# A new timetable for the side work of an attention and spiking feed-forward kernel

## The chip, the core and the metric

The kernel runs on one core of a Trainium2 chip. A core has five engines that run their own instruction streams and meet only through semaphores: TensorE (PE, matrix products into PSUM), VectorE (DVE), ScalarE (ACT), GpSimd (POOL) and SyncE (SP, here only a DMA queue). Data lie in SBUF (128 partitions) and in PSUM (eight banks of 128 x 512 floats). The metric is the device time of one launch in microseconds, lower is better; it is given as the median of several runs.

## What is computed

For each of 32 sequences of 256 tokens and 128 features, in f32:

```python
xn  = layernorm(x)
h   = layernorm(xn) * ln_scale + ln_bias
c_q, c_kv = h @ w_down_q.T, h @ w_down_kv.T            # 64 latents each
q, k, v = (c_q @ w_up_q.T), (c_kv @ w_up_k.T), (c_kv @ w_up_v.T)   # 16 heads of 64
q, k = rope(q), rope(k)
attn = softmax(q @ k.T / 8)                            # 256 x 256 for each head
att_out = (attn @ v) @ w_out.T + xn
y   = relu(xn @ W_fc.T)**2 @ W_proj.T                  # 512 hidden units
spikes = number of firings in 5 steps of a leaky integrator driven by y, / 5
out = x + att_out + spikes
```

The top-k of the reference's attention is computed there but not returned, and is not needed.

## The kernel before

A sequence is a batch b; its 16 heads are 8 pairs. One step handles one pair at each stage of a software pipeline, so there are 32 x 8 = 256 steps, plus 12 to fill the pipeline and 8 to drain it. In the text a step has the number p = 0 to 7 within its batch, and g is the running number of the pair. The table `LEAD` says how far ahead of the current pair each stage works: project 12, rope 10, scores 8, turn 7. Each engine has a function `step(i, s)` that issues its part of one step in a fixed order written out by hand, and `run` calls it: some steps written out ahead, a loop whose body is two batches (16 steps), then the last body and the drain written out.

The main stages of one step, engine by engine:

- PE: `scores` of pair g+8 (8 matmul records into one of two halves of ps_s), `project` of pair g+12 (into the one bank ps_qk, from the latents of that batch, once ACT has copied the pair before out of it), the side work (`extras`), and `weigh_latents` of pair g (8 records into the one bank ps_u).
- DVE: `row_max` of g+8, `rotate` of g+12 (times the cosines, ps_qk to qk), side work, `turn` of g+7 (32 x 32 transposes of the exponentials), side work.
- ACT: `exponentials` of g+8 (four of them), `copy_projected` of g+12 (ps_qk to raw), in every odd step `exchange` (two DMAs that swap neighbouring rows of two pairs, raw to partner), side work, `copy_u` of g.
- POOL: `add_rotated` of g+10, two instructions (partner times the sines; added to qk), then side work. It waits for the exchange by DMA of its two pairs. In step p it handles pair p+10, so the pairs 16 and 17, exchanged by ACT in step 5, are POOL's in steps 6 and 7, and PE needs them for the scores of steps 0 and 1 of the batch after.
- SP: after the turn of every fourth pair (in steps 0 and 4), `move`: 16 DMAs of 128 KB, turned to gathered, which `weigh_latents` reads four steps later.

The side work of a batch, with the step p in which each engine has it before the change:

- The input chain works two batches ahead: load x (SP 0), `moments_of` (DVE 0), `inverse_std` (POOL 0), `normalise` twice (ACT 1), `transpose_inputs` (PE 2), `copy_inputs` (ACT 2), `latents` (PE 3), `lead_latents` (ACT 3), `split_latents` (DVE 3); the first `project` that reads the result is PE's in step 4. `residual` (POOL 3) adds x to xn in place.
- `latents_by_token` of batch b+1 (PE 1) and `copy_latents` (ACT 1).
- Feed forward: `ffn_in` half 0 of b+1 (PE 7) and half 1 of b (PE 0), `relu` (ACT 7, 0), `square` (POOL 1, 2), `ffn_out` (PE 4, 5), `integrate` (DVE 5, 6).
- Softmax sums: `invert_sums` (DVE 4), `split_sums` (POOL 5), `transpose_rden` (PE 7), `copy_rden` (ACT, first of step 0 of the batch after), then `broadcast_rden` and `normalise_u` of that batch's steps 0 to 3.
- Output of batch b-1: `attention_out` in four parts (PE 4, 5, and two in 6), `add_spikes` (DVE 7), `transpose_sum` (PE 7), `finish` (DVE 7), `store` (SP).

All input and feed-forward products share the one bank ps_a; the sums and the output share ps_b.

## Time and profile before

| | |
|---|---|
| median of 3 runs (lowest to highest) | 1379.97 us (1379.85 to 1381.91) |
| the profiled execution | 1372.12 us, its span 1370.3 us |
| mean granted TensorE clock | 0.951 of 2.4 GHz |
| busy: PE, DVE, ACT, POOL | 81%, 72%, 61%, 59% of the span |
| DMA engines, mean busy share and rate | 62% in the steady part, 159 GB/s over the span |
| one batch in the steady part | 41.0 us |

The profiled execution is a run of its own and 7.9 us shorter than the median. Busy shares are unions of instruction records; PE's matmul records overlap, so its share is an upper reading. A record of f32 matrix products comes twice, since the product is issued as two instructions. The timeline of a stretch gives for each engine the start of an instruction and, in brackets, how long the engine had been idle before it and what ended that; the time an instruction holds its engine is best read from one start to the next start, since the records of neighbouring instructions overlap by some 0.1 us.

### The profile page before, as it was taken

How to read it: one execution, taken by the hardware profiler on the slowest of the kernel's cores; microseconds unless marked ns; L12 is line 12 of the kernel's file. 1: busy time of each engine (PE TensorE's matmuls, PEld its weight loads, DVE VectorE, ACT ScalarE, POOL GpSimd, SP SyncE). 2: the span in 40 equal slices, each digit the busy share in tenths (PEclk: the TensorE clock that was granted, in tenths of full speed). 3: DMA queues.
4: the chain of work that ended last, by engine and by line, in shares of the span. 5: the costliest groups of instructions: out<-in, count | busy, mean ns of one | idle time of the engine just before them, and what ended most of it. 6: DMA issues, size and time to landing. Idle time of an engine off the chain costs nothing.

```text
span 1370.3 us, 25645 instructions
## 1 busy us (share of the span) xinstructions
PE 1103.4 (81%) x6880; PEld 741.2 (54%) x6880; DVE 981.3 (72%) x1350; ACT 840.0 (61%) x2945; POOL 806.7 (59%) x837
## 2 busy tenths in 40 slices
PE   3677788887788887788887788887788887788886
PEld 2445555555555555555555555555555555555554
DVE  3667777677777777777677777676778676778672
ACT  2566666666665666665666665666665666666650
POOL 3567656557656557656556656556656556755640
PEclk9889999999999999999999999999999999999998
DMA  4456665665665665665665675565575565576562
GB/s 143 119 149 162 183 169 149 178 159 147 176 174 147 173 162 149 171 178 149 167 168 146 168 180 154 160 172 148 162 180 159 155 173 151 158 181 162 153 171 54
DMA packets 93273, 217.87 MB, mean 159 GB/s; under 512 B 22464, under 2 KB 43200, under 8 KB 93120
## 3 DMA queue, kind: packets, MB, share of 16 engines
q1 hardware_dynamic: 72768, 150.45, 47.1%
q10 hardware_dynamic: 20480, 67.13, 13.2%
q8 instruction: 11, 0.18, 0.1%
q14 instruction: 14, 0.11, 0.0%
HBM read 7.77 MB, written 4.19 MB: 9 GB/s over the span
## 4 chain that ended last, share of the span: by engine, by line
PE 37%; issue 17%; ACT 16%; DVE 15%; ACTq 7%; POOL 5%; SPq 1%; DMA 1%; DVEq 0%; POOLq 0%
PE ps_s L300 9%; PE ps_u L314 9%; ACT prob L473 9%; DVE neg_max L596 7%; ACTq L493 7%; PE ps_b L390 6%; PE ps_a L365 4%; ACT raw L485 3%; PE ps_qk L290 3%; DVE turned L605 3%; POOL partner L730 2%; PE ps_a L352 2%; POOL qk L733 2%; DVE count L649 2%; DVE qk L591 2%
## 5 line engine op out<-in xcount | busy, mean ns | idle before, releaser
L473 ACT ACTIVATE prob<-ps_s,neg_max 128x256 f32<-128x256 f32 x1024 | 472.3, 476 | 308.2 <-DVE neg_max L596 308.2
L730 POOL TENSOR_TENSOR partner<-partner,rope_sb 128x512 f32<-128x512 f32 x256 | 326.9, 1277 | 472.9 <-DMA partner<-raw 472.3
L596 DVE TENSOR_REDUCE neg_max<-ps_s 128x4 f32<-128x1024 f32 x256 | 312.2, 1220 | 203.0 <-PE ps_s L300 201.0
L733 POOL TENSOR_TENSOR qk<-qk,partner 128x512 f32<-128x512 f32 x256 | 325.7, 1272 | 20.1
L605 DVE STREAM_TRANSPOSE turned<-prob 128x1024 f32<-128x1024 f32 x256 | 314.1, 1227 | 0.9
L300 PE MATMUL ps_s<-qk 64*128 64x256 f32 x2048 | 296.5, 409 | 13.8 <-POOL qk L733 12.4
L314 PE MATMUL ps_u<-gathered,ckv 128*64 128x256 f32 x2048 | 280.6, 395 | 5.7 <-DMA gathered<-turned 3.7
L290 PE MATMUL ps_qk<-latent,wup_hi 128*128 128x256 f32 x512 | 173.4, 358 | 123.5 <-DVE latent L638 98.5
L300 PEld LDWEIGHTS ps_s<-qk 64*128 64x128 f32 x2048 | 179.6, 189 | 126.6 <-issue 80.1
L290 PEld LDWEIGHTS ps_qk<-latent,wup_hi 128*128 128x128 f32 x512 | 105.5, 206 | 215.2 <-issue 149.5
L473 ACT ACTIVATION_READ_ACCUMULATOR prob<-ps_s,neg_max 128x1 f32 x1024 | 211.1, 206 | 0.0
L314 PEld LDWEIGHTS ps_u<-gathered,ckv 128*64 128x64 f32 x2048 | 125.1, 137 | 115.2 <-issue 69.2
L591 DVE TENSOR_TENSOR qk<-ps_qk,rope_sb 128x512 f32<-128x512 f32 x256 | 174.2, 681 | 8.9 <-PE ps_qk L291 8.7
L485 ACT COPY raw<-ps_qk 128x512 f32<-128x512 f32 x256 | 153.4, 599 | 9.1 <-DVE qk L591 9.1
L390 PE MATMUL ps_b<-u_n,wvo_sb 128*128 128x256 f32 x512 | 154.4, 443 | 0.8 <-DVE u_n L619 0.8
L291 PE MATMUL ps_qk<-latent,wup_lo 128*128 128x256 f32 x512 | 144.4, 301 | 0.0
L501 ACT COPY u_raw<-ps_u 128x256 f32<-128x256 f32 x256 | 98.8, 386 | 68.0 <-issue 39.9
L390 PEld LDWEIGHTS ps_b<-u_n,wvo_sb 128*128 128x128 f32 x512 | 107.3, 226 | 16.4 <-issue 2.1
L619 DVE TENSOR_TENSOR u_n<-u_raw,ps_b 128x512 f32<-128x512 f32 x128 | 86.9, 679 | 32.6 <-PE ps_b L382 32.6
L291 PEld LDWEIGHTS ps_qk<-latent,wup_lo 128*128 128x128 f32 x512 | 107.9, 211 | 0.0
L638 DVE TENSOR_TENSOR latent<-ps_a,latent 64x256 fp32r<-64x256 f32 x64 | 27.0, 422 | 101.5 <-ACT latent L527 101.1
L382 PE MATMUL ps_b<-rden_t,sel_sb 128*128 128x256 f32 x256 | 55.5, 298 | 41.4 <-ACT rden_t L545 38.8
(57 smaller groups left out, 906.3 us busy)
## 6 DMA issues: line engine op xcount, KB each, us to landing
gathered<-turned SPq DMA_DIRECT2D x1024, 128.0 KB, 2.8
partner<-raw ACTq DMA_DIRECT2D x256, 256.0 KB, 2.6
x_sb<-in_x SPq DMA_DIRECT2D x32, 128.0 KB, 2.2
resid<-xn_sb SPq DMA_DIRECT2D x32, 128.0 KB, 2.0
out<-out_sb SPq DMA_DIRECT2D x32, 128.0 KB, 1.9
turned<-in_wup SPq DMA_DIRECT2D x2, 512.0 KB, 5.8
rope_sb<-in_rope SPq DMA_DIRECT2D x1, 512.0 KB, 6.9
turned<-in_wo_t SPq DMA_DIRECT2D x1, 512.0 KB, 8.2
```

The source lines that it names most:

```text
L290: nc.tensor.matmul(bank, wup_hi[:, which, cols], rhs, start=True, stop=False)
L291: last = nc.tensor.matmul(bank, wup_lo[:, which, cols], rhs, start=False, stop=True)
L300: last = nc.tensor.matmul(ps_s[:, s % 2, h, t, :], qk[rows, s % 4, 0, t * P:(t + 1) * P], qk[rows, s % 4, 1, :], start=True, stop=True)
L314: last = nc.tensor.matmul(ps_u[h * L:(h + 1) * L, 0:S], ckv[:, (s // PAIRS) % 2, kt, :], gathered[:, (s // GROUP) % 2, :, s % GROUP, h, kt ...
L390: last = nc.tensor.matmul(ps_b[:, 0:S], wvo_sb[:, pair, :], u_n[:, pair, :], start=(pair == 0), stop=(pair == PAIRS - 1))
L473: last = nc.scalar.activation(prob[:, s % 2, :, h, :, t, :].rearrange("p j k c -> p k j c"), ps_s[:, s % 2, h, t, :].rearrange("p (k j c) ...
L485: nc.scalar.copy(raw[:, duo % 2, s % 2, :, :], ps_qk[:, :, :]).then_inc(raw_ready, 1)
L591: nc.vector.tensor_tensor(qk[:, s % 4, :, :], ps_qk[:, :, :], cos_sb, ALU.mult).then_inc(cos_ready, 1)
L596: nc.vector.tensor_reduce(neg_max[:, s % 2, :, :], ps_s[:, s % 2, :, :, :], AXIS_X, ALU.max, negate=True).then_inc(max_ready, 1)
L605: nc.vector.transpose(turned[:, par, :, s % GROUP, :], prob[:, s % 2, :, :, :, :, :].rearrange("p j h k t c -> p j (h k t c)"))\
L730: nc.gpsimd.tensor_tensor(other, other, sin_sb, ALU.mult).then_inc(sin_ready, 1)
L733: nc.gpsimd.tensor_tensor(qk[:, s % 4, :, :], qk[:, s % 4, :, :], other, ALU.add).then_inc(rope_done, 1)
```

## The change

The side work gets new steps, the order within a step changes in places, and four buffers change with it.

- Input chain: now three batches ahead at its head. `load_x` of b+3 (SP 0), `moments_of` b+3 (DVE 2), `inverse_std` (POOL 3), `normalise` (ACT 4 and 5, one each), `transpose_inputs` b+3 (PE 7), `copy_inputs` (ACT 7), then of b+2: `latents` (PE 0), `lead_latents` (ACT 0), `split_latents` (DVE 1). `residual` of b+2 moves to POOL 4.
- `latents_by_token` and `copy_latents` of b+1 move from step 1 to step 0, into another part of ps_a.
- Feed forward: `ffn_in` of b+1 in PE 5 and 6, `relu` ACT 5 and 6, `square` POOL 6 and 7, `ffn_out` PE 2 and 3, `integrate` DVE 3 and 4.
- Sums: `invert_sums` from DVE 4 to 5, `split_sums` from POOL 5 to 6 (behind `square`, and behind `add_rotated`, which stands first in POOL's step). `transpose_rden` stays in PE 7.
- Output: `attention_out` one part in each of steps 4 to 7; `finish` is the first thing of DVE's step 0 of the batch after; `store` and `keep_residual` in SP 3. `broadcast_rden` comes behind the other extras of its step.
- Buffers: h_t gets two halves; `residual` writes a new buffer `early`, not xn_sb in place. Waits are added to match (`latent_split`, `relu_done`, `ckv_ready`, `ckv_mm`, `moments_ready`, `res_ready`).
- Prologue: the statistics of x of batch 1 (`moments_of`, `inverse_std`) are made there. The loop runs one body less and the last two bodies are written out; the drain has nine steps.

The core of the diff:

```diff
@@ run
-            with eng.Fori(1, B // UNROLL - 1) as i:
+            with eng.Fori(1, B // UNROLL - 2) as i:
...
-            for s in range(PAIRS):
+            for s in range(PAIRS + 1):
@@ SP step
-                if p == 0:
-                    if not outside(b, B):
-                        sp.wait_ge(res_ready, done(b))
-                    if not outside(b, B) and not outside(b + 2, B):
-                        load_x(b + 2, b0)
+                if p == 0 and not outside(b + 1, B) and not outside(b + 3, B):
+                    sp.wait_ge(res_ready, done(b + 1))
+                    load_x(b + 3, 1 - b0)
+                if (s + turn) % GROUP == GROUP - 1 and not outside(g + turn, STEPS):
+                    move(g + turn, s + turn)
+                if p == 3:
...
@@ PE extras
+                if not outside(b - 1, B) and p >= 4:
+                    attention_out(b - 1, p - 4)
+                if p == 0:
+                    if not outside(b + 2, B):
+                        latents(b + 2, b0)
+                    if not outside(b + 1, B):
+                        latents_by_token(b + 1, 1 - b0)
+                if not outside(b, B) and p in (2, 3):
+                    ffn_out(b, p - 2)
+                if not outside(b + 1, B) and p in (5, 6):
+                    ffn_in(b + 1, p - 5, 1 - b0)
+                if p < 4 and not outside(b - 1, B):
+                    broadcast_rden(b - 1, p)
+                if p == 7:
+                    if not outside(b + 3, B):
+                        transpose_inputs(b + 3, 1 - b0)
+                    if not outside(b - 1, B):
                         transpose_sum(b - 1)
...
                     if not outside(b, B):
                         transpose_rden(b)
@@ ACT step
+                if p == 0:
+                    if not outside(b + 2, B):
+                        lead_latents(b + 2, b0)
+                    if not outside(b + 1, B):
                         copy_latents(b + 1, 1 - b0)
+                if not outside(b + 1, B) and p in (5, 6):
+                    relu(b + 1, p - 5)
+                if not outside(b + 3, B):
+                    if p in (4, 5):
+                        normalise(b + 3, 1 - b0, p - 4)
                     elif p == 7:
...
+                        copy_inputs(b + 3, 1 - b0)
@@ DVE step
+                if p == 0 and not outside(b - 2, B):
+                    finish(b - 2, b0, i - 1)
...
-                if p == 0 and not outside(b + 2, B):
-                    moments_of(b + 2, b0, i + 1)
-                elif p == 3 and not outside(b + 2, B):
+                if p == 1 and not outside(b + 2, B):
                     split_latents(b + 2, b0)
-                elif p == 4 and not outside(b, B):
+                elif p == 2 and not outside(b + 3, B) and not outside(b + 1, B):
+                    moments_of(b + 3, 1 - b0, i + 1 + b0)
+                elif p == 5 and not outside(b, B):
                     invert_sums(b, b0)
...
-                    if p == 5:
+                    if p == 3:
                         for k in (0, 1):
                             integrate(b, b0, k)
-                    elif p == 6:
+                    elif p == 4:
@@ POOL step
                 if not outside(g + LEAD["rope"], STEPS):
                     add_rotated(g + LEAD["rope"], s + LEAD["rope"], i)
-                if p == 0 and not outside(b + 2, B):
-                    inverse_std(b + 2)
-                if p in (1, 2) and not outside(b, B):
-                    square(b, p - 1)
-                if p == 3 and not outside(b + 2, B):
-                    residual(b + 2, b0)
-                if p == 5 and not outside(b, B):
+                if p == 3 and not outside(b + 3, B) and not outside(b + 1, B):
+                    inverse_std(b + 3)
+                if p == 4 and not outside(b + 2, B):
+                    residual(b + 2, b0, i + 1)
+                if p in (6, 7) and not outside(b + 1, B):
+                    square(b + 1, p - 6)
+                if p == 6 and not outside(b, B):
                     split_sums(b)
```

## Rows read from the trace of the kernel before

**Rows 1.** The page: busy time and share of the span of each engine.
```profile
PE 1103.4 (81%) x6880; PEld 741.2 (54%) x6880; DVE 981.3 (72%) x1350; ACT 840.0 (61%) x2945; POOL 806.7 (59%) x837
```

**Rows 2.** Instructions of copy_rden, one in each batch: first and last start.
```profile
L545 ACT CAST rden_t<-ps_b x9: 390/390/391, 354.6 to 682.3; 128x256 fp32r<-128x256 f32 x9
```

**Rows 3.** Who waited for whom over the whole span: total us, times, longest.
```profile
PE ps_qk L290 <- DVE latent L638: 98.5, 32, 3.3
```

**Rows 4.** Timeline, steps 2 to 4: start, duration, engine, line, [idle before].
```profile
693.05 0.41 PE L326 MATMUL ps_a<-ident_sb,z_sb 128*128 128x128 f32 x2 [2.09 <-ACT z_sb L513]
...
701.44 0.86 DVE L638 TENSOR_TENSOR latent<-ps_a,latent 64x256 fp32r<-64x256 f32 x2 [3.22 <-ACT latent L527]
...
702.43 0.58 PE L290 MATMUL ps_qk<-latent,wup_hi 128*128 128x256 f32 x1 [3.21 <-DVE latent L638]
```

**Rows 5.** Stretches of 2 us: busy of PE, PEld, DVE, ACT, POOL, then clock, DMA, GB/s.
```profile
692.00:694.00 2.00, 0.95 (x8) 0.74 (x10) 1.29 (x2) 2.00 (x8) 0.00 (x0) 1.00 0.98 240
...
702.00:704.00 2.00, 1.57 (x6) 1.49 (x7) 1.94 (x3) 0.00 (x0) 1.73 (x3) 0.58 0.00 0
```

**Rows 6.** Timeline, PE: end of step 4, and step 5 without a wait.
```profile
706.40 1.08 PE L314 MATMUL ps_u<-gathered,ckv 128*64 128x256 f32 x8
707.41 1.13 PE L300 MATMUL ps_s<-qk 64*128 64x256 f32 x8
708.48 0.38 PE L290 MATMUL ps_qk<-latent,wup_hi 128*128 128x256 f32 x1
...
709.05 1.02 PE L390 MATMUL ps_b<-u_n,wvo_sb 128*128 128x256 f32 x4
...
710.87 1.08 PE L314 MATMUL ps_u<-gathered,ckv 128*64 128x256 f32 x8
711.88 1.13 PE L300 MATMUL ps_s<-qk 64*128 64x256 f32 x8
```

**Rows 7.** Timeline, DVE, step 6.
```profile
713.07 1.23 DVE L596 TENSOR_REDUCE neg_max<-ps_s 128x4 f32<-128x1024 f32 x1 [0.73 <-PE ps_s L300]
714.21 0.68 DVE L591 TENSOR_TENSOR qk<-ps_qk,rope_sb 128x512 f32<-128x512 f32 x1
714.80 1.24 DVE L605 STREAM_TRANSPOSE turned<-prob 128x1024 f32<-128x1024 f32 x1
715.96 1.30 DVE L649 SCALAR_TENSOR_TENSOR count<-ps_a,count 128x256 f32<-128x256 f32 x3
```

**Rows 8.** Timeline, ACT, step 5 and the first exponential of step 6.
```profile
709.85 0.47 ACT L473 ACTIVATE prob<-ps_s,neg_max 128x256 f32<-128x256 f32 x1 [1.88 <-DVE neg_max L596]
...
711.67 0.60 ACT L485 COPY raw<-ps_qk 128x512 f32<-128x512 f32 x1
712.29 1.12 ACTq L493 DMA_DIRECT2D partner<-raw  x2
713.46 0.37 ACT L501 COPY u_raw<-ps_u 128x256 f32<-128x256 f32 x1 [1.19 <-issue]
714.33 0.48 ACT L473 ACTIVATE prob<-ps_s,neg_max 128x256 f32<-128x256 f32 x1 [0.50 <-DVE neg_max L596]
```

**Rows 9.** Timeline: the move of step 4 on SP, POOL, and PE's transpose_rden.
```profile
697.99 1.04 POOL L770 TENSOR_TENSOR relu_sb<-relu_sb 128x512 f32<-128x512 f32 x1
...
706.88 5.58 SPq L245 DMA_DIRECT2D gathered<-turned  x9
...
707.63 0.21 POOL L762 CAST rden_hl<-rden 128x32 fp32r<-128x32 f32 x1
707.92 0.25 POOL L764 TENSOR_TENSOR rden_hl<-rden,rden_hl 128x32 fp32r<-128x32 f32 x1
...
717.88 1.28 POOL L730 TENSOR_TENSOR partner<-partner,rope_sb 128x512 f32<-128x512 f32 x1 [9.71 <-DMA partner<-raw]
...
718.23 0.38 PE L374 MATMUL ps_b<-ident_sb,rden_hl 128*128 128x128 f32 x2
...
719.23 1.28 POOL L733 TENSOR_TENSOR qk<-qk,partner 128x512 f32<-128x512 f32 x1
```

**Rows 10.** The exchange DMAs over two batches: from issue to landing.
```profile
DMA to landing us min/median/max: 2.2/2.7/5.2
```

More of the change, by code:

```diff
@@ L270, in step @@
                     if not outside(b, B):
+                        sp.wait_ge(res_ready, done(b))
                         keep_residual(b0)
[L272 to L273 removed]
             run(sp, prologue, step)
```

96 lines of the change are left out of this document (32 added, 64 removed).

## Prediction, made before the run

> **What bounds the kernel now.** I read the busy shares first: PE 81%, DVE 72%, ACT 61%, POOL 59% [rows 1]. No engine is full, so the time is set by who waits for whom. Next I took the spacing of an instruction that comes once in a batch: eight periods in 327.7 us, 40.96 us a batch [rows 2]. The table of waits names the largest wait of PE: project behind the latents of the next batch but one, 98.5 us in 32 times, so 3.1 us in every batch [rows 3]. The timeline shows the place: in step 3 the products of the latents, their copy on ACT and their split on DVE follow one another within one step; the split starts at 701.44, after DVE has been idle for 3.22 us, and PE's project of step 4 at 702.43, after 3.21 us [rows 4]. In the same way PE stood 2.09 us in step 2 for the normalised input [rows 4].
>
> The wait costs more than itself. After it TensorE's clock is at the lower of its two levels: 0.58 in the stretch from 702 to 704 [rows 5]. The same work (project, one part of attention_out, half of ffn_out) takes 3.97 us from 702.43 to 706.40 [rows 4, 6], and in the next step, at the full clock, 2.39 us from 708.48 to 710.87 [rows 6]. So 1.6 us more, 4.8 us in all. After the shorter wait of 2.09 us the clock stayed at 1.00 [rows 4, 5].
>
> Then I read a step without such a wait, from start to start. PE: scores 1.07, project 0.57, two groups of four side products 1.82, weigh 1.01; 4.47 in all from 707.41 to 711.88 [rows 6]. DVE: row_max 1.14, rotate 0.59, turn 1.16 [rows 7]. ACT: four exponentials 1.82, then the copy of the projection; the copy with the exchange behind it holds ACT for 1.79, without one about 0.48 (the 0.60 record less the overlap of 0.1) [rows 8]. From scores' start to row_max is 1.19 [rows 6, 7], from row_max to the first exponential 1.26 [rows 7, 8].
>
> **The change part by part.** Hardly any work is added or taken away: no product, no exponential. What changes is who waits. I lay the new order out by hand for one batch, with these durations, and put zero at the start of row_max in step 1.
>
> DVE leads in steps 1 to 4. Step 1 has row_max, rotate, normalise_u (as long as rotate, 0.6) and the split (0.86 [rows 4]) and the turn: 1.14 + 0.6 + 0.6 + 0.9 + 1.2 = 4.4. Step 2 has the moments instead of the split; their instructions don't stand in my rows, and I take 0.8, the split's price (at least 0.4, the price of one small DVE instruction, at most 1.3, that of three compares [rows 7]): 4.4. Step 3 has two compares of integrate, at 1.30 / 3 = 0.43 each [rows 7]: 4.4. Step 4 has three and no normalise_u: 4.2. So row_max of step 5 is at 17.4. PE's own load is 2.9 to 3.8 in these steps, with ffn_out and broadcast in steps 2 and 3, and ACT's at most 3.9; both fit beneath DVE. The latents are split in step 1 and read in step 4, three steps of slack, so the wait of 3.21 us and the slow clock behind it go. The input is normalised in steps 4 and 5 and transposed in 7, so the 2.09 us wait goes as well. This is the gain: 3.2 + 1.6 + 2.1 = 6.9 us of PE in a batch, before one asks what is late next.
>
> Next comes ACT. In step 5 it has exponentials 1.8, copy with exchange 1.8, a relu 0.5, a normalise of two instructions 0.8 and copy_u 0.25: 5.15. It begins at 17.4 + 1.3 = 18.6 and is free at 23.8, where the maxima of step 6 have been ready since 22.8. That 1.0 us is the first new wait. PE's weigh of step 6 needs copy_u of step 5 and ends at 25.0.
>
> PE in step 7: scores to 26.1, project 0.6, the last part of attention_out 0.86, transpose_inputs 0.6, a wait of 0.2 for add_spikes, transpose_sum 0.2. It comes to transpose_rden at 28.6. If rden were there, the next step's first scores would end at 31.0, the load of PE's step 0 (1.07 + 0.57 + 0.43 + 0.48 + 0.24 + 1.1, with a wait of 0.4 for copy_inputs) would follow, and row_max of the next step 1 would be at 35.4. That is a batch of 35.4 us.
>
> But rden isn't there. This is the step on which I settle. split_sums moves on POOL from step 5 to step 6 and so behind add_rotated of pair 16 and behind a square. POOL handles its instructions in order, and add_rotated of pair 16 waits for the exchange which ACT issues in step 5, in the middle of the 16 DMAs of the move of step 4. Now the rows: the move began at 706.88, the copy of the projection at 711.67, the exchange at 712.29, and POOL could start only at 717.88, after 9.71 us idle [rows 8, 9]. That is 6.2 us after the copy, where a landing of the median 2.7 instead of 5.2 [rows 10] would give 3.7. In the kernel before split_sums had been done at 708.2, while POOL waited for nothing; PE's transpose_rden at 718.23 came before POOL was through with pair 16, at 720.5 [rows 9]. With the old spacing of steps the new place of split_sums alone would be some 4 us too late.
>
> In my timetable: row_max of step 5 at 17.4, exponentials 18.6, copy 20.4, POOL on pair 16 at 26.6 (the exchange falls 4.7 us into the move; before 5.4 us, so as contended), 2.6 for the two instructions (717.88 to 719.23 and 1.28 [rows 9]), 29.2; square 1.0 [rows 9], 30.2; split_sums 0.54 (707.63 to 708.17 [rows 9]), 30.8. PE has then waited 2.2 us. It goes on: transpose 0.3, weigh 1.0, so step 0 starts at 32.1; its load is 3.9 (the wait for copy_inputs is covered now); 36.0; row_max of step 1 1.2 later, 37.2. The chain closes, and DVE, free at 36.9, isn't late. A batch of 37.2 us.
>
> POOL's other dates: pair 12 is contended in the same way by the move of step 0 (copy of step 1 at 3.1, POOL at 9.2, done 11.8; scores want it at 10.9, but DVE takes them only at 13.1, which hides it: free, and up to 1 us a batch if DVE were faster). inverse_std in step 3 then ends at 16.6, just as ACT's normalise comes at 16.7; 0.8 us of slack on ACT hides a late one. SP: load_x and its wait for residual stand ahead of the move of step 0, but the residual was added in step 4 of the batch before, so the move isn't held. store and keep_residual come behind the move, done issuing at about 10 (16 DMAs at 0.62 [rows 9]), and residual needs the copy at 19. The move itself is issued at -0.3 and read at 14; it took about 11 us before, so 3 us of slack. Added semaphore waits on DVE (moments_ready, ckv_ready) and ACT (ckv_mm, res_ready) are for things one step or more old: 0 each, at most 0.1 for each of the four. One body written out more costs nothing that I can see; I put 0 to 3 us in all on it.
>
> Sum. Taking 0.2 for the small handovers, 37.4 us against 40.96 in each of 30 batches (pairs of the batches 0 to 29; in the last two no exchange is left in step 5): 106 us. In the filling steps one wait of 4.8 goes, and the moments of batch 1 in DVE's prologue add 0.8: 4 us less. The drain is one step longer but has the same chain: 0, up to 2 either way. 1372.1 - 110 = 1262 for a profiled execution; the median of the runs stood 7.9 above that before, so 1270.
>
> **The rivals.**
>
> A, the forecast: 1270, with its own range 1250 to 1290 (a landing 0.6 us earlier or later for each batch is 18 us). For it: the 9.71 us idle of POOL ahead of exactly that pair.
>
> B: the new wait of 2.2 us in step 7 pulls TensorE's clock to its lower level. The rows have a wait of 2.09 us that didn't and one of 3.21 us that did [rows 4, 5]; mine lies nearer the first. The price is the 1.6 us from above: 39.0 us a batch, 1318. The Trainium skill (TensorE: Matmul & The Clock Gate, section Why this matters for your kernels) warns against idle gaps between bursts of matmuls since they send the clock back to 1.2 GHz; by that rule this timetable is at risk wherever it leaves one long gap, and the trace bears the rule out at 702 us.
>
> C: the exchange isn't held up, since the moves lie otherwise, and rden is in time: 35.4 us a batch, 30 x 5.55 + 4 = 170 less, 1210. Against it: both contended exchanges of a batch had the same delay, at 3.6 and 5.4 us into a move. The Trainium skill (DMA: Bandwidth & Descriptors, section Issuing engines are not separate DMA queues) says the DMAs of all issuing engines run on the same 16 engines and interleave, which leaves no room for C unless the move is over.
>
> D, slower than before: the exchange of step 5 is served only when the move has drained. In the rows its end at 717.88 is 11.0 us after the move's start, which could be the move's own end. Then it lands 11 - 4.7 + 2.7 = 9.0 us after its issue instead of 5.6, PE waits 5.6 us, the clock falls (1.6): 37.4 + 3.4 + 1.6 = 42.4 us, 1420. It turns the sign from about 2.1 us more delay on, if the clock falls too. Against it: the other contended exchange of the same batch was through while the DMA engines were still full.
>
> E: the waits only change their names and nothing is gained; 1380. Nothing in the load of the engines (at most about 31 us in a batch) speaks for it.
>
> **How the numbers follow.** A 0.64, B 0.17, C 0.12, D 0.05, E 0.02. The predicted time is A's, 1270. Range 1235 to 1330: A and B with room for the unknown costs; C and D stay out. A measurement of this kernel can tell about 0.2% from no change. Faster by more than that 0.91 (all but D, E and a rest of B), within it 0.02, slower 0.07.
>
> **What the profile should show.** The wait of project for the latents and its clock of 0.58 gone; the mean clock at 0.98 or more (B: about 0.95); a wait of PE at transpose_rden (L374's successor) for POOL's second instruction of split_sums, some 2.2 us, about 30 times; POOL still idle ahead of pair 16 for the exchange; DVE's wait for scores mostly in steps 7, 0 and 1. In steps 1 to 4 steps of 4.2 to 4.4 us with DVE nearly full, about 5.1 on ACT in step 5, and a batch of 37.4 us. It would be wrong if transpose_rden doesn't wait (C), if the wait is over 3 us (B, D), or if DVE isn't the leader of steps 1 to 4.

## The result and the profile after

The changed kernel takes 1252.76 us, the median of 4 runs (1250.01 to 1256.78), against 1379.91 us (1379.67 to 1381.91) for the kernel before. The ratio is 0.908 with the interval 0.905 to 0.910. Predicted were 1270 us, with a range of 1235 to 1330, and 1250 to 1290 for the forecast by itself. The profiled execution took 1253.07 us; its span is 1251.3 us and the mean granted clock 0.982, where it was 0.951.

The page of the profile after, busy time and share of the span of each engine, answers to [rows 1]. DVE, ACT and POOL work as long as before, within 1.1 us; their shares have risen since the span is shorter.

```profile
PE 1074.8 (86%) x6880; PEld 712.4 (57%) x6880; DVE 982.4 (79%) x1350; ACT 840.9 (67%) x2945; POOL 807.0 (64%) x837
```

The table of waits after (total us, times, longest) answers to [rows 3]. Project's wait for the split of the latents, 98.5 us in 32 times before, is left once, with 2.4 us. In its place stand PE's waits for POOL's second instruction of split_sums, 30 times and 43.6 us, so 1.45 us in a batch. Project's waits for ACT's copy of the pair before have grown from 25.0 to 58.1 us.

```profile
POOL partner L727 <- DMA partner<-raw: 353.8, 68, 8.7
...
DVE neg_max L589 <- PE ps_s L302: 159.9, 106, 8.5
...
PE ps_qk L292 <- ACT raw L481: 58.1, 99, 3.5
...
PE ps_b L377 <- POOL rden_hl L763: 43.6, 30, 5.7
```

The timeline of one batch after (start, duration, engine, line, and in brackets the idle time before) shows the chain that the prediction had laid out by hand. It answers to [rows 8, 9]. ACT copies the projection in step 5 at 612.37 and issues the exchange; the move of step 4 has been running since 608.33; POOL gets the exchanged pair only at 618.45; then come its second instruction, a square and split_sums; and transpose_rden on PE starts at 622.62, after an idle of 1.58 us.

```profile
608.33 10.95 SPq L247 DMA_DIRECT2D gathered<-turned  x16
...
612.37 0.60 ACT L481 COPY raw<-ps_qk 128x512 f32<-128x512 f32 x1
613.00 1.22 ACTq L489 DMA_DIRECT2D partner<-raw  x2
...
618.45 1.28 POOL L727 TENSOR_TENSOR partner<-partner,rope_sb 128x512 f32<-128x512 f32 x1 [3.79 <-DMA partner<-raw]
619.81 1.27 POOL L730 TENSOR_TENSOR qk<-qk,partner 128x512 f32<-128x512 f32 x1
621.04 1.03 POOL L769 TENSOR_TENSOR relu_sb<-relu_sb 128x512 f32<-128x512 f32 x1
622.03 0.20 POOL L761 CAST rden_hl<-rden 128x32 fp32r<-128x32 f32 x1
622.31 0.25 POOL L763 TENSOR_TENSOR rden_hl<-rden,rden_hl 128x32 fp32r<-128x32 f32 x1
...
622.62 0.44 PE L377 MATMUL ps_b<-ident_sb,rden_hl 128*128 128x128 f32 x2 [1.58 <-POOL rden_hl L763]
```

To see where the time went I took the start of every row_max on DVE, from that of pair 16 to that of pair 240 (28 batches), and worked out the mean length in us of each of the eight steps, from one row_max to the next. The step lengths and batches of all the other kernels below are taken over the same 28 batches. Steps count as in the kernel's description; "hand" is the timetable of the prediction, each step rounded by itself.

| step | 0 | 1 | 2 | 3 | 4 | 5 | 6 | 7 | batch |
|---|---|---|---|---|---|---|---|---|---|
| before | 5.28 | 3.49 | 6.12 | 7.81 | 4.95 | 4.47 | 4.47 | 4.32 | 40.92 |
| after | 3.87 | 4.61 | 4.29 | 4.25 | 4.11 | 4.19 | 4.72 | 6.87 | 36.91 |
| hand | 3.9 | 4.4 | 4.4 | 4.4 | 4.2 | 4.1 | 4.7 | 7.2 | 37.2 |

The gain comes from steps 2, 3, 0 and 4 (1.8, 3.6, 1.4 and 0.8 us); 1.1 us are given back in step 1, which took over the split, and 2.5 in step 7, where PE waits for the sums. 4.01 us a batch, 30 times, are 120 us; the profiled executions differ by 119.

### The profile page after: what moved, and what is told of

It reads as the page before. It is cut to its first block, busy times and chain, and to the rows that moved or that the text cites. A ratio compares the mean times of both kernels' runs of the same rounds, so it can differ in the third digit from the quotient of the medians.

```text
span 1251.3 us, 25664 instructions
## 1 busy us (share of the span) xinstructions
PE 1074.8 (86%) x6880; PEld 712.4 (57%) x6880; DVE 982.4 (79%) x1350; ACT 840.9 (67%) x2945; POOL 807.0 (64%) x837
## 3 DMA queue, kind: packets, MB, share of 16 engines
HBM read 7.77 MB, written 4.19 MB: 10 GB/s over the span
## 4 chain that ended last, share of the span: by engine, by line
issue 46%; POOL 37%; DVE 7%; PE 6%; SPq 1%; POOLq 1%; DMA 1%; DVEq 0%; ACT 0%; ACTq 0%
POOL partner L727 17%; POOL qk L730 10%; POOL relu_sb L769 4%; POOL rstd L742 2%; POOL early L753 2%; PE ps_u L316 2%; DVE turned L598 2%; DVE neg_max L589 2%; PE ps_s L302 1%; DVE u_n L612 1%; DVE qk L584 1%; PE ps_b L393 1%; SPq L247 1%; DMA x_sb<-in_x 1%; POOL var_eps L737 1%
## 5 line engine op out<-in xcount | busy, mean ns | idle before, releaser
L730 POOL TENSOR_TENSOR qk<-qk,partner 128x512 f32<-128x512 f32 x256 | 326.2, 1274 | 20.1
L292 PE MATMUL ps_qk<-latent,wup_hi 128*128 128x256 f32 x512 | 162.7, 340 | 65.8 <-ACT raw L481 58.1
L292 PEld LDWEIGHTS ps_qk<-latent,wup_hi 128*128 128x128 f32 x512 | 98.4, 192 | 162.6 <-ACT raw L481 131.1
L393 PE MATMUL ps_b<-u_n,wvo_sb 128*128 128x256 f32 x512 | 134.7, 387 | 0.8 <-DVE u_n L612 0.8
L293 PE MATMUL ps_qk<-latent,wup_lo 128*128 128x256 f32 x512 | 134.8, 285 | 0.0
L293 PEld LDWEIGHTS ps_qk<-latent,wup_lo 128*128 128x128 f32 x512 | 99.5, 194 | 0.0
L393 PEld LDWEIGHTS ps_b<-u_n,wvo_sb 128*128 128x128 f32 x512 | 89.8, 193 | 11.8 <-issue 2.9
L355 PE MATMUL ps_a<-xn_t,wfc_sb 128*128 128x256 f32 x256 | 69.9, 396 | 1.5 <-ACT relu_sb L533 1.4
L385 PE MATMUL ps_b<-rden_t,sel_sb 128*128 128x256 f32 x256 | 66.0, 339 | 4.1 <-DVE u_n L612 2.6
```

Of the source, the lines that this page charges most:

```text
L292: nc.tensor.matmul(bank, wup_hi[:, which, cols], rhs, start=True, stop=False)
L293: last = nc.tensor.matmul(bank, wup_lo[:, which, cols], rhs, start=False, stop=True)
L393: last = nc.tensor.matmul(ps_b[:, 0:S], wvo_sb[:, pair, :], u_n[:, pair, :], start=(pair == 0), stop=(pair == PAIRS - 1))
L730: nc.gpsimd.tensor_tensor(qk[:, s % 4, :, :], qk[:, s % 4, :, :], other, ALU.add).then_inc(rope_done, 1)
```

## The experiments

Twelve kernels were run, each beside the kernel before, whose medians in these comparisons were 1378.8 to 1380.1 us. Seven of them leave out or change a part of the computation (the moves cut short, and the experiments in which PE reads the latents or the input of the batch before), so they are good for timing only. The theory to be tested has two parts: that after is set by the chain exchange, POOL, split_sums, PE in step 7, and that the gain came from taking the waits of the input chain out of the steps 2 and 3. Rivals: that the wait in step 7 is only the last of several limits, so that nothing comes of removing it; and that the slow clock, not the wait, is what costs.

### split_sums one step earlier

```diff
-                if p == 6 and not outside(b, B):
+                if p == 5 and not outside(b, B):
                     split_sums(b)
```

> The changed kernel with one edit: split_sums goes back from step 6 to step 5 on POOL, ahead of the pair whose exchange is late. In the changed kernel PE waits 0.7 to 2.0 us in step 7 of each batch for it (43.6 us in all). Theory A (that wait stands on the path that sets the end): the wait of PE at transpose_rden goes from the table of waits, the batch falls from 36.95 to about 35.5 us, the time to 1205 to 1225. Rival (the scores of the next batch's first pair, which need the same late exchange, or ACT's step 5 take its place): less than 0.5 us a batch is gained, 1238 to 1253.

Measured: 1208.23 us (1205.13 to 1209.98), ratio to before 0.876 (0.874 to 0.879). The timeline of PE in this kernel, around transpose_rden, has it right behind transpose_sum, with no idle time:

```profile
631.73 0.44 PE L400 MATMUL ps_b<-ident_sb,acc_t 128*128 128x128 f32 x2 [0.23 <-DVE acc_t L653]
632.01 0.38 PE L377 MATMUL ps_b<-ident_sb,rden_hl 128*128 128x128 f32 x2
```

Step 7 falls from 6.87 to 5.17 us, the batch from 36.91 to 35.58. The hand timetable without the wait had 35.4, and the prediction gave 1210 for rden in time. So the wait of PE costs after 44.5 us, and one line gives it back. This kernel is faster than both.

### The moves cut to a quarter of their bytes

```diff
-                        sp.dma_start(gathered[32 * block_of:32 * block_of + 32, par, rows, :, :, :, :, :],
-                                     turned[32 * rows:32 * rows + 32, par, block_of, :, :]).then_inc(moved[par], 16)
+                        sp.dma_start(gathered[32 * block_of:32 * block_of + 32, par, rows, 0:1, :, :, :, :],
+                                     turned[32 * rows:32 * rows + 32, par, block_of, 0:1, :]).then_inc(moved[par], 16)
...
```

What is cut from this diff fills gathered with zeros once, in the prologue. The kernel leaves out three quarters of the exponentials.

> The changed kernel, but each of the 16 DMAs of a move carries only the first of four pairs, 32 KB instead of 128 KB, so three quarters of the gathered exponentials are left out (gathered is filled with zeros once). Theory A (the exchange is late since it shares the DMA engines with the move): from the copy of the projection in step 5 to POOL's start on pair 16 it is about 3.7 us instead of 6.1, split_sums is in time without being moved, the wait at transpose_rden is under 0.3 us, the time 1205 to 1225. Rival (POOL or ACT is late for a reason of its own): the 6.1 us stay, and the time stays within 5 us of 1253.

Measured: 1203.17 us (1202.35 to 1204.19), ratio 0.873 (0.871 to 0.875). split_sums still stands in step 6 here, and yet PE waits for it only once, in the first batch. The timeline of ACT, POOL and PE in and behind step 5 shows what changed: POOL starts 4.1 us after the copy (622.36 to 626.44) and not 6.1 us (612.37 to 618.45 after). Over the 28 batches the means are 4.11 and 5.77. The expectation had 3.7; the exchange is not quite as fast as one outside a move, for in the kernel before the pairs that ACT exchanges in step 7 take 3.59 in the mean. It is just enough: POOL is through with split_sums at 630.56, and PE comes to transpose_rden at 630.80.

```profile
622.36 0.59 ACT L487 COPY raw<-ps_qk 128x512 f32<-128x512 f32 x1
622.98 1.16 ACTq L495 DMA_DIRECT2D partner<-raw  x2
...
626.44 1.27 POOL L733 TENSOR_TENSOR partner<-partner,rope_sb 128x512 f32<-128x512 f32 x1 [2.92 <-DMA partner<-raw]
...
630.31 0.25 POOL L769 TENSOR_TENSOR rden_hl<-rden,rden_hl 128x32 fp32r<-128x32 f32 x1
...
630.80 0.38 PE L383 MATMUL ps_b<-ident_sb,rden_hl 128*128 128x128 f32 x2
```

So the origin of the wait is shown from both ends: with the reader moved ahead of the delayed work, and with the delay itself cut down. The 5 us by which this kernel beats the last fit the same cause: PE's scores wait for POOL's add_rotated 1.3 us in all here, and 26.1 us in the last.

### The same step in the kernel before

```diff
-                if p == 5 and not outside(b, B):
+                if p == 6 and not outside(b, B):
                     split_sums(b)
```

> The kernel before with one edit of the change alone: split_sums from step 5 to step 6 on POOL. Theory A (the new place is late by itself, behind the pair whose exchange is late): PE waits 2.5 to 3.5 us in step 7 for POOL, and as ACT's copy_rden was 1.2 us late already, 1.5 to 3 us a batch come on top: 1425 to 1470. Rival (the place costs nothing in the kernel before, only the shorter step makes it late): 1378 to 1385.

Measured: 1511.77 us (1505.13 to 1518.93), ratio 1.096 (1.091 to 1.102), clock 0.883: slower by 133 us, more than the 45 to 90 that I had given it. The table of waits has the new one, and the windows (us, then busy time of the engines, POOL's last, then the granted clock) show what it does 30 times over:

```profile
PE ps_b L374 <- POOL rden_hl L764: 81.7, 30, 3.8
```

```profile
702.00:704.00 2.00, 0.80 (x6) 0.56 (x6) 1.78 (x3) 0.78 (x3) 1.92 (x2) 1.00 0.84 186
704.00:706.00 2.00, 0.87 (x3) 0.82 (x4) 0.00 (x0) 1.63 (x7) 1.92 (x4) 0.68 0.22 62
706.00:708.00 2.00, 2.00 (x8) 1.03 (x8) 1.58 (x2) 0.44 (x1) 1.56 (x2) 0.50 0.62 244
```

Step 7 is 8.35 us instead of 4.32, of which the wait itself is 81.7 / 30 = 2.7; step 2 is 7.65 instead of 6.12, and step 0 gives 1.0 back. What I left out was the clock: it falls behind the new wait (0.68 and 0.50 in the rows), and in 23 of the 28 batches it falls in step 2 as well, where it never did before. The move of split_sums by itself is a loss of 133 us, inside a change that gains 127.

### Before, with project cut loose from the split

```diff
+   back = 0 if isinstance(g, int) and g < PAIRS else 1
...
-   pe.wait_ge(latent_split, done(i * UNROLL + s // PAIRS))
+   pe.wait_ge(latent_split, done(i * UNROLL + s // PAIRS - back))
...
-   bank, rhs = ps_qk[:, which, :], latent[:, (s // PAIRS) % 2, which, :]
+   bank, rhs = ps_qk[:, which, :], latent[:, (s // PAIRS - back) % 2, which, :]
```

> The kernel before with the dependence of project on the latents relaxed by a batch: from batch 1 on, project reads the latents of the batch before (a part of the computation that is changed, so queries and keys are another sequence's); every instruction stays where it is. Theory A (the chain of the latents in step 3 is the main loss, 3.2 us of wait and 1.6 us of slow clock): the wait and the stretch at clock 0.58 go, 3.5 to 4.8 us a batch, 1231 to 1272, near the changed kernel's 1253. Rival (the wait is a symptom, another engine is as late at that point): less than 1.5 us a batch, above 1333.

Measured: 1376.67 us (1373.43 to 1381.05, 10 runs), ratio 0.999 (0.997 to 1.000). The largest wait of PE in the kernel before is gone and nothing is gained that can be told from noise: the theory fell. The timeline of DVE tells why step 3 stays as long as it was:

```profile
698.68 1.22 DVE L597 TENSOR_REDUCE neg_max<-ps_s 128x4 f32<-128x1024 f32 x1 [3.49 <-PE ps_s L301]
...
704.32 0.86 DVE L639 TENSOR_TENSOR latent<-ps_a,latent 64x256 fp32r<-64x256 f32 x2 [3.21 <-ACT latent L528]
```

DVE works in the order in which its instructions were issued. In step 3 it stands for 3.21 us at split_latents, and the turn and row_max of step 4 are queued behind; row_max can't come before 706.48, 7.80 us after that of step 3, exactly as before. PE, now free, only comes early to wait elsewhere: of the 98.5 us, project's waits for ACT's copy take up 57 (25.0 before, 82.4 here), ffn_out's for the split 36 (none before), and those for rden_t 7 (38.8 and 46.2). The row that names PE's wait was right, but DVE was held by the same data, with the next row_max behind it. And the slow clock, which I had booked as a part of this wait, shows up elsewhere. In the kernel before it falls in step 3 in each of the 28 batches and never in step 2; here it falls in step 2 in 17 of them and never in step 3. It does so behind a wait (2.07 us at 694.93) like the one behind which it had stayed up in the batch of [rows 4, 5]. Step 4 is 1.8 us shorter, but step 2 is 1.2 longer, step 5 0.7 and step 0 0.2, and nothing is left of it. Why the clock now falls in step 2 isn't shown. The windows around that wait:

```profile
696.00:698.00 2.00, 2.00 (x13) 1.30 (x10) 0.00 (x0) 2.00 (x9) 0.70 (x1) 0.60 0.96 252
698.00:700.00 2.00, 2.00 (x11) 1.44 (x8) 1.32 (x2) 0.46 (x3) 1.92 (x3) 0.55 0.93 201
```

### The split one step later as well

```diff
-                elif p == 3 and not outside(b + 2, B):
-                    split_latents(b + 2, b0)
-                elif p == 4 and not outside(b, B):
-                    invert_sums(b, b0)
+                elif p == 4:
+                    if not outside(b + 1, B) and not outside(b + 2, B):
+                        split_latents(b + 2, b0)
+                    if not outside(b, B):
+                        invert_sums(b, b0)
```

> The last experiment on the kernel before (project one batch behind in its latents, which changes a part of the computation) with one edit more: split_latents one step later on DVE, in step 4 behind row_max and rotate. There project's wait was gone, but DVE still stood 3.2 us in step 3 with the split at the head of its queue, and row_max of step 4 behind it. Theory A2 (it is DVE's own wait in its order, and not project's, that made step 3 7.8 us long): step 3 falls to 4.5 to 5.5 us, ffn_out waits about 1 us for the split in step 4, 1.5 to 3 us a batch are gained, 1288 to 1335. Rival (step 3 is held by something else): less than 0.5 us a batch, above 1362.

Measured: 1326.71 us (1325.00 to 1330.56), ratio 0.963 (0.960 to 0.966). Within the expectation, and 50 us less than the kernel without this second edit: it was DVE's wait that had to go. Against the kernel before, step 3 falls from 7.81 to 3.65 us, further than I had expected. But step 2 rises from 6.12 to 7.46, since PE's wait for the normalised input (below) is still there and the clock now falls behind it in 26 of the 28 batches, and step 4 rises from 4.95 to 6.18, where ffn_out has to wait for the split (38.0 us in 30 times):

```profile
711.91 0.66 PE L327 MATMUL ps_a<-ident_sb,z_sb 128*128 128x128 f32 x2 [2.15 <-ACT z_sb L514]
```

### After, with the slack of the split taken away

```diff
-                if p == 1 and not outside(b + 2, B):
+                if p == 0 and not outside(b + 2, B):
                     split_latents(b + 2, b0)
```

> The changed kernel with one step of slack taken back: split_latents on DVE in step 0, the step in which ACT copies the latents, instead of step 1. Theory A2 (the slack at the change of engine is what pays): DVE stands about 1.9 us in step 0 for ACT's copy, the split's 0.9 us move from step 1 to 0, so the batch grows by 1 to 2 us: 1283 to 1313. Rival (the slack is not needed once the chain is spread over more steps): within 6 us of 1253.

Measured: 1380.76 us (1373.83 to 1387.79, 10 runs), ratio 1.002 (0.999 to 1.005). One step of slack removed at one handover of DVE, and the whole gain of the change is gone; I had expected a quarter to a half of it. The timelines of DVE and PE, and the windows, show the sequence:

```profile
655.17 0.86 DVE L634 TENSOR_TENSOR latent<-ps_a,latent 64x256 fp32r<-64x256 f32 x2 [2.17 <-ACT ckv L528]
```

```profile
661.13 0.58 PE L292 MATMUL ps_qk<-latent,wup_hi 128*128 128x256 f32 x1 [3.52 <-ACT raw L481]
```

```profile
658.00:660.00 2.00, 0.00 (x0) 0.00 (x0) 2.00 (x4) 1.33 (x6) 0.00 (x0) 1.00 0.68 152
660.00:662.00 2.00, 0.87 (x4) 0.87 (x5) 2.00 (x2) 1.08 (x5) 0.00 (x0) 0.55 0.91 207
662.00:664.00 2.00, 2.00 (x7) 1.64 (x7) 0.70 (x2) 1.65 (x8) 0.00 (x0) 0.50 0.92 262
664.00:666.00 2.00, 2.00 (x11) 0.96 (x9) 1.12 (x4) 1.03 (x5) 0.00 (x0) 0.50 1.01 283
```

DVE stands 2.17 us for the latents, which delays row_max, and with it ACT's exponentials and copy of the projection, and PE is idle for 3.52 us; towards the end of that its clock falls to the lower level and stays there until after 666. A wait of 2.2 us on DVE costs 41.22 - 36.91 = 4.3 us a batch.

### The second normalise in step 6, then in step 7

Both start from the kernel with split_sums in step 5. The first:

```diff
-                    if p in (4, 5):
-                        normalise(b + 3, 1 - b0, p - 4)
+                    if p in (4, 6):
+                        normalise(b + 3, 1 - b0, (p - 4) // 2)
```

> A version meant to beat both: split_sums in step 5, and the second normalise of ACT from step 5 (the fullest of ACT, 5.2 us, which delays the exponentials of step 6 and copy_u, for which PE waits) to step 6. Theory: 0.2 to 0.5 us a batch on top of the first edit (1208): 1193 to 1203. Rival (the next limit stands at the same height): 1205 to 1211.

Measured: 1208.52 us (1205.53 to 1210.35), ratio 0.877 (0.874 to 0.879), the same as the 1208.23 without it. My theory that ACT's long step 5 costs time fell: step 6 stays at 4.73 (4.71 before the edit), step 7 gives up 0.14 and step 0 takes 0.18. The timeline of PE shows why. It works through step 6 without a gap, 4.68 us from scores to scores; over the 28 batches PE is idle for 0.02 us in this step, and for 0.01 in the kernel after, where the normalise still stands in step 5. The step is as long as PE's own work.

```profile
623.97 1.13 PE L302 MATMUL ps_s<-qk 64*128 64x256 f32 x8
...
627.64 1.08 PE L316 MATMUL ps_u<-gathered,ckv 128*64 128x256 f32 x8
628.65 1.13 PE L302 MATMUL ps_s<-qk 64*128 64x256 f32 x8
```

The second puts normalise into the step in which PE reads it:

```diff
-                    if p in (4, 5):
-                        normalise(b + 3, 1 - b0, p - 4)
-                    elif p == 7:
+                    if p in (4, 7):
+                        normalise(b + 3, 1 - b0, (p - 4) // 3)
+                    if p == 7:
                         copy_inputs(b + 3, 1 - b0)
```

> As the first edit (split_sums in step 5), but the second normalise of ACT in step 7, the step in which PE transposes its result, so without a step of slack; work and all else as before. PE then waits in step 7 for ACT behind its exponentials, exchange and normalise. Theory A2: a wait of 3.5 to 4.5 us in each batch, and as it is longer than 3.2 us, TensorE's clock falls to the lower level behind it (mean clock 0.94 to 0.96), 4 to 6 us a batch against 1208: 1328 to 1390. Rival on the clock (it stays at the higher level): 3 to 4.3 us, 1298 to 1335, mean clock 0.98 or more.

Measured: 1372.74 us (1369.55 to 1376.50, 10 runs), ratio 0.995 (0.993 to 0.997), within the expectation. 164 us are lost by two ACT instructions two steps later. PE waits 4.55 us for them in the batch shown, and its clock is at 1.2 GHz for 6 us there; it falls in each of the 28 batches, in most of them for a shorter time:

```profile
642.26 0.68 PE L329 MATMUL ps_a<-ident_sb,z_sb 128*128 128x128 f32 x2 [4.55 <-ACT z_sb L508]
```

```profile
640.00:642.00 2.00, 0.00 (x0) 0.00 (x0) 0.00 (x0) 0.85 (x2) 1.92 (x3) 0.50 0.49 195
642.00:644.00 2.00, 1.74 (x8) 1.57 (x8) 0.00 (x0) 0.62 (x3) 1.92 (x2) 0.50 0.17 68
644.00:646.00 2.00, 2.00 (x10) 0.77 (x8) 0.42 (x1) 0.24 (x1) 1.92 (x3) 0.50 0.00 0
```

Step 7 is 11.02 us instead of 5.17. From normalise to the step in which PE transposes its result the changed kernel has two steps. One is as good; none costs 164 us.

### Before, with the transposed input cut loose too

```diff
-                pe.wait_ge(xn_ready, done(n))
-                pe.wait_ge(z_ready, done(n))
+                back = 0 if isinstance(n, int) and n == 0 else 1
+                pe.wait_ge(xn_ready, done(n - back))
+                pe.wait_ge(z_ready, done(n - back))
...
-                for src, at in ((z_sb[:, :, :], 0), (xn_sb[:, par, :, :], S)):
+                par = (par + back) % 2
+                for src, at in ((z_sb[:, par, :, :], 0), (xn_sb[:, par, :, :], S)):
```

> The last of the experiments on the kernel before (latents of the batch before, split in step 4: 39.5 us a batch) with PE's wait in step 2 gone as well: transpose_inputs turns the normalised input of the batch before (z_sb gets two halves; a further part of the computation that is changed), so it no longer waits 2.1 us for ACT's normalise of the same step, and the clock has no wait of 2 us to fall behind. All instructions stay in their steps. Theory A3 (the three places without a step of slack, and the clock that falls behind one of them, are nearly all that the change wins; moving feed forward and sums is worth little by itself): 2.6 to 3.8 us a batch, 1212 to 1250, at or below the changed kernel's 1253, mean clock 0.98 or more. Rival (the moved feed forward and sums carry a part of the gain): above 1270.

This comes on top of the last edits; what is cut from the diff gives z_sb two halves and adds waits on ACT and POOL that keep the buffers apart. Measured: 1290.75 us (1288.85 to 1302.96), ratio 0.937 (0.931 to 0.943). The wait of 2.15 us is gone, and 36 us with it, but that is 41 to 79 us short of what I had expected. The time lies where the rival had put it; its reason, the moved feed forward and sums, isn't shown by that. Weigh of step 2 now waits 1.16 us for copy_u, which on ACT stands behind the exchange, a copy and both normalises, and in 7 of the 28 batches the clock still falls in this step, as in the one shown:

```profile
685.85 1.21 PE L315 MATMUL ps_u<-gathered,ckv 128*64 128x256 f32 x8 [1.16 <-ACT u_raw L506]
686.99 2.08 PE L301 MATMUL ps_s<-qk 64*128 64x256 f32 x8
...
689.00 0.58 PE L291 MATMUL ps_qk<-latent,wup_hi 128*128 128x256 f32 x1
```

```profile
686.00:688.00 2.00, 2.00 (x12) 1.18 (x12) 0.00 (x0) 2.00 (x10) 0.10 (x1) 0.67 0.92 266
688.00:690.00 2.00, 2.00 (x10) 1.34 (x7) 0.89 (x1) 1.11 (x4) 1.92 (x2) 0.50 0.95 205
```

### The normalises taken out of ACT's step 1

```diff
-                    if p == 1:
-                        normalise(b + 2, b0, 0, i + 1)
+                    if p == 4:
                         normalise(b + 2, b0, 1, i + 1)
                     elif p == 2:
                         copy_inputs(b + 2, b0)
+                        normalise(b + 2, b0, 0, i + 1)
```

> e9_apart3 with ACT's two normalises moved out of step 1: that of the xn input into step 2 (behind copy_inputs), that of z into step 4. As in e9 every batch is projected from the latents, and transposes the input, of the batch before, so only the timing is meant. Theory R (the rest of e9 lies in ACT's step 1): in e9 the exchange, the copy of ckv and the two normalises stand ahead of copy_u in ACT's step 1; copy_u starts at 685.45, weigh behind it at 685.85 after an idle of 1.16 us, TensorE's clock falls, scores of step 2 take 2.01 us instead of 1.07, and row_max comes at 689.11. Without the two normalises weigh follows the transposes at about 684.5, scores end at 686.6, row_max is at 686.7: 2.4 us a batch less, 30 x 2.4 = 72, so about 1219; range 1205 to 1240. Rival: the clock falls behind what is left of waits (0.65 for ckv, 1.28 for the split of the latents, 1.12 for rden_t) and the time comes back there: above 1265.

Measured: 1274.02 us (1272.38 to 1276.47), ratio 0.923 (0.921 to 0.925), clock 0.985. The time lies in the range of the rival (above 1265) and not in mine (1205 to 1240), but the rival's clock isn't the reason: here it falls in none of the 28 batches. The step in question is 4.54 us long in the timeline (row_max at 714.59 and 719.13) where it was 6.98 (682.13 and 689.11), 2.44 less for an expected 2.4. But the 2.4 was read from one of the 7 batches in which the clock had fallen (7.36 us in the mean; the other 21 have 5.82). Over the 28 batches the step loses 1.59 (6.20 to 4.61), and the next one gains 1.14 (3.79 to 4.93), since a new wait stands there. The rows of POOL and of PE name it:

```profile
673.41 11.15 SPq L245 DMA_DIRECT2D gathered<-turned  x16
...
677.04 1.12 ACTq L498 DMA_DIRECT2D partner<-raw  x2
...
682.64 1.28 POOL L737 TENSOR_TENSOR partner<-partner,rope_sb 128x512 f32<-128x512 f32 x1 [3.89 <-DMA partner<-raw]
684.00 1.27 POOL L740 TENSOR_TENSOR qk<-qk,partner 128x512 f32<-128x512 f32 x1
```

```profile
685.32 1.13 PE L301 MATMUL ps_s<-qk 64*128 64x256 f32 x8 [1.31 <-POOL qk L740]
```

It is the other contended exchange, that of pair 12 inside the move of step 0. (The scores which the expectation puts into step 2 are PE's first work of step 3.)

### copy_latents ahead of the exchange

```diff
+                if p == 1 and not outside(b + 1, B):
+                    copy_latents(b + 1, 1 - b0)
                 if (s + LEAD["project"]) % 2 == 1 and not outside(g + LEAD["project"], STEPS):
                     exchange(g + LEAD["project"], s + LEAD["project"])
```

> e10_apart3_norms with copy_latents ahead of the exchange in ACT's step 1, not behind its two DMA issues, so that PE's transposes needn't wait for the shared bank (0.65 us in e9, of which the whole is the 1.26 us that ACT takes for the issues). The computation is left out in the same way as in e9. Theory: another 0.65 us a batch, 20 us less than e10, so 1185 to 1220 if R holds. Rival: the exchange goes out 0.3 us later and the waits of steps 3, 4 and 7 set the time: within 6 us of e10.

Measured: 1274.09 us (1272.08 to 1274.92), ratio 0.923 (0.921 to 0.925): no gain, the rival. PE's wait of 0.65 us is gone, and that for POOL has gone from 1.31 to 1.36 in the batches looked at, from 46.8 to 51.0 us in all; step 2 is 0.54 us shorter and step 3 0.64 longer.

### The moves cut short there too

The same edit of `move` as above, on top of the last kernel.

> e11_apart3_norms_ckv with the move's 16 DMAs cut from 128 KB to 32 KB each (a quarter of the weights reaches gathered, which is zero elsewhere; besides, as in e9, the latents and the input of the batch before are used). e10 and e11 gained 17 us of the 72 and 92 that I had expected of them together with e9: row_max of step 3 comes 2.4 us sooner, but scores of step 4 then wait 1.31 us for POOL's add_rotated of pair 12, whose exchange (issued at 677.04 in e10) falls into the move of step 0 (from 673.41, 11.15 us) and lets POOL start only at 682.64, 5.6 us later. Theory X (the contended exchange of ACT's step 1 is what came next and took the rest of the gain): with short moves that exchange lands 2.7 us sooner, the wait of 1.3 us a batch goes, and that of 0.3 us for pair 16 ahead of step 7; 30 x 1.6 = 48 us, so about 1226; range 1212 to 1243. Rival: the split of the latents ahead of ffn_out (1.3) and rden_t (1.1 to 1.25) hold the batch where it is, or the clock falls: above 1260.

Measured: 1230.10 us (1229.53 to 1230.71), ratio 0.892 (0.890 to 0.894). The expectation was 1226. In the table of waits scores stand behind POOL once, for 1.8 us; they did so 43 times and for 51.0 us in the last kernel. Step 3 falls from 5.57 to 4.08 us. PE's waits that the rival named are all still there:

```profile
PE ps_b L393 <- ACT rden_t L557: 46.6, 32, 1.8
...
PE ps_a L376 <- DVE latent L650: 37.7, 30, 2.0
...
PE ps_s L307 <- POOL qk L746: 1.8, 1, 1.8
```

So the exchange in the midst of the move held back most of the gain of the two kernels before it, 44 us. The rest of the 92 us expected of them was in part never there, since the 2.4 us a batch was 1.6 in the mean.

## Why the prediction was right, step by step

**The order of the chain.** Right, and shown by two experiments (split_sums one step earlier, and the short moves): the copy of step 5, the contended exchange, pair 16, square, split_sums, transpose_rden. From the copy to POOL I had 6.2 us (6.08 in the batch shown, 5.77 in the mean), from there to the end of split_sums 4.2 (4.11, 618.45 to 622.56). The dates relative to row_max of step 1 add up to a batch of 37.2; it is 36.91.

**The wait at transpose_rden.** Its place and its cause were right, its size of 2.2 us was an over-estimate: 1.45 in the mean. Counted from row_max of step 7, which the hand timetable has at 17.4 + 4.1 + 4.7 = 26.2 and the batch shown at 618.25: PE reaches transpose_rden 2.8 us later (621.04, that is 622.62 less the idle of 1.58) where I had 28.6 - 26.2 = 2.4, and POOL is through with split_sums after 4.3 (622.56) where I had 30.8 - 26.2 = 4.6. The two errors of 0.3 to 0.4 us add up to the 0.7. Step 7 is 6.87 for 7.2.

**Steps led by DVE.** Right: 4.61, 4.29, 4.25, 4.11 against 4.4, 4.4, 4.4, 4.2. The moments, which I took at 0.8 for want of a row, hold DVE for 0.82 (635.99 to 636.81 in the timeline).

**ACT in step 5.** The lateness itself was right: ACT begins on the maxima of step 6 at 615.85, 2.35 us after their row_max began at 613.50, and not 1.26, so it is 1.1 us late for the 1.0 forecast. That step 6 is 4.7 us long because of it was not: PE has no idle time there, with the normalise in step 5 or without, and the step is PE's own work of 4.7. The match of 4.7 and 4.72 is in part luck: the timetable had weigh of step 6 behind ACT's copy_u, and PE's own work by [rows 6] at 4.5.

**The gain.** I counted 3.2 + 1.6 + 2.1 us of PE as what goes. The sum was taken from the timetable and didn't rest on it. As an account of the gain it is the step that failed. The experiments show that these waits can't be booked one by one: the 3.2 of project bring nothing alone (1376.67), 1.6 us a batch with DVE's wait for the same data gone too (39.32 for 40.92), and the slow clock that I had tied to this wait moves to a shorter one. With the transposed input and the normalises moved too it is 3.3 us a batch (37.58 for 40.92), and the short moves give another 1.3 (37.70 to 36.44).

**The sum.** 106 us for 30 batches should have been 30 x 4.01 = 120. For the filling I had a gain of 4 us, and beside these 120 there is none: the profiled executions differ by 119. And 7.9 us went on top for the median of the runs over the profiled execution; in the kernel after the two agree within 0.3 us (1252.76 and 1253.07), so the 7.9 seems to belong to one execution before. 14 - 5 + 8 is the 17 us by which 1270 is too high.

**The rivals.** B, that the clock falls behind the new wait, happens now and then: in 5 of 29 batches (all but the first that waits there) the clock was at the lower level behind transpose_rden. Four of these last 37.8 to 38.3 us from one transpose_rden to the next, the others 36.1 to 37.2; the fifth runs into the drain. Two windows of the kernel after, one with and one without, stand below; the waits before them are 1.55 us (at 360.51) and 1.58 us (at 622.62). By the difference of the means, 1.3 us, it costs some 6 us in all, an estimate. C is what one line more would give (1208.23 for 1210). The closeness of these two is in part luck: the profiled executions differ by 163.7 us where C had 170, and the same 7.9 us make up for it. D and E have nothing for them: the exchange was served during the move, not behind it.

```profile
362.00:364.00 2.00, 2.00 (x10) 1.19 (x8) 0.00 (x0) 0.74 (x2) 2.00 (x3) 0.50 0.14 57
...
624.00:626.00 2.00, 2.00 (x16) 1.60 (x15) 0.82 (x1) 0.65 (x2) 2.00 (x2) 1.00 0.18 72
```

**What the change is made of.** The move of split_sums is a loss (133 us in the kernel before, 44.5 in the one after); the slack on the side of the split and the normalise is worth the whole gain (128 us when taken from the split of the kernel after, 164 us when taken from the normalise of the kernel with split_sums in step 5). The loss is hidden inside the gain. What the moved feed forward is worth by itself wasn't tried; between the kernel before with its three waits cut loose (1274) and the kernel after with split_sums in step 5 (1208) lie 66 us. In the table of waits of the former stand PE's waits for the split ahead of ffn_out, 39.3 us, and for rden_t in step 0, 39.7 us; the latter has none of the first and 1.5 us of the second. That the feed forward and the relus moved out of these steps are the reason was only argued.

## What to carry to other kernels

Lay out the changed order by hand from the durations of single instructions, engine by engine, and ask of each moved step what stands ahead of it in its engine's queue; that gave every step here within 0.4 us (step 6 for another reason than mine), while the waits removed add up to 6.9 us for a gain of 4.0. A wait in the table is named at its victim: before it is counted as a gain, look whether another engine waits for the same data with the rest of its step queued behind it. A handover between engines within one step can cost twice the wait itself once the matmul clock falls behind it, so one step of slack at each is cheap; but of every step that is moved for it, check whether a DMA that is delayed by a larger one stands ahead.

## What the runs showed of the hardware

- **The clock.** It isn't the length of the one wait that decides. Behind waits of 1.55 and 1.58 us the same code ran at 1.2 GHz once and at 2.4 GHz the other time. In the 29 batches of the kernel after that were counted above, it fell behind waits of 1.05 us (at 1173.15) and of 1.55 to 1.86 us, and stayed up behind one of 1.96 us (at 140.53). A wait of 2.09 us left the clock up in the kernel before [rows 5], and the wait in that place did so in each of its 28 batches; one of 2.07 us in the same place went with a fall once PE's later wait was gone, in 17 of 28 batches. Behind waits of 0.65 and 1.16 us within one step it fell in 7 of 28 batches. What decides between the first two the rows don't show: PE's records ahead of both are the same. The Trainium skill (TensorE: Matmul & The Clock Gate, section Why this matters for your kernels) warns of idle gaps between bursts of matmuls. The trace agrees that the clock falls behind gaps, and adds that gaps well below 2 us can be enough, in some batches and not in others.
- **The price of a removed or added wait.** It isn't fixed. 2.7 us of new wait went with 4.7 more a batch (45.65 for 40.92), 2.2 us on DVE with 4.3, with the slow clock on top in both; and a wait of 3.2 us removed was worth nothing.
- **Two streams of DMAs.** The exchange of 512 KB in step 5 took 5.45 us from its issue to POOL's start inside a move (613.00 to 618.45) and 3.46 with moves of a quarter of the bytes (622.98 to 626.44), with the same number of DMAs in the queues; it is mostly the bytes, not the count. The Trainium skill (DMA: Bandwidth & Descriptors, section Issuing engines are not separate DMA queues) says that DMAs of all issuing engines share the engines; the trace agrees. In the kernel before, from ACT's copy to POOL's start, it is 6.20 us in the mean in step 5, inside a move of 2 MB, and 3.59 in step 7, outside one: 2.6 us for the move.
